# Choosing each expert's first tokens from 512 packed words, a longer lag in a routing pipeline, and a reordered pair of loads, in a two-layer kernel on Trainium2

## What is computed

```python
# block 0
xn = layernorm(x)
s  = two transformer layers (attention, MLP) of xn, per sequence
logits = xn @ router_w.T                      # 64 experts, top 8 of each token
pos = cumsum(onehot, axis=0) - 1              # place of a token in its expert's queue
valid = pos < 64                              # an expert takes its FIRST 64 tokens
g = silu(routed(valid tokens) + shared)
x = x + s * g
# block 1
xn = layernorm(x)
topk_ids = argmax(xn @ gate_w); score = sigmoid(max)   # 32 experts, top 1
order = argsort(topk_ids)                     # tokens sorted by expert
d = grouped_mm(silu(sorted @ wg) * (sorted @ wu), wd)
x = x + linear_attention(xn) * silu(shared(xn) + d[inverse order])
```

## Time and profile before

| | us |
|---|---|
| three runs | 1530.03, 1534.50, 1534.76 (median 1534.5) |
| the profiled execution, its own time | 1530.27 |
| its span, first to last instruction | 1528.4 |
| PE busy | 1209.7 (79%) |
| PE weight loads busy | 912.8 (60%) |
| DVE busy | 1069.0 (70%) |
| ACT busy | 787.0 (51%) |
| POOL busy | 653.9 (43%) |
| mean granted TensorE clock | 0.909 |

### The profile page before, as it was taken

How to read it: one execution, slowest core, us unless ns; L and a number is a source line. 1 busy time by engine, 2 the same in 40 slices (tenths; PEclk the granted TensorE clock), 3 DMA queues, 4 the chain that set the end, 5 groups by cost and what they waited for, 6 DMA issues and landing times. The chain is left out here.

```text
span 1528.4 us, 29193 instructions
## 1 busy us (share of the span) xinstructions
PE 1209.7 (79%) x7783; PEld 912.8 (60%) x7784; DVE 1069.0 (70%) x3641; ACT 787.0 (51%) x2010; POOL 653.9 (43%) x1270
## 2 busy tenths in 40 slices
PE   3999999999600899999999744568888888698883
PEld 2777777778500677777777533346666666355552
DVE  3777777777697677777777367757777777266663
ACT  1666576665300565665665455646666656233331
POOL 3344343443100354554555456714444433155555
PEclk9999999999855999999999855579999999699997
DMA  3432433424100122122122155534444443355552
GB/s 130 143 133 87 143 103 120 139 88 147 40 0 24 42 58 57 39 60 55 39 61 48 18 167 183 164 131 142 144 148 148 154 155 125 99 165 151 161 167 76
DMA packets 159336, 162.58 MB, mean 106 GB/s; under 512 B 21030, under 2 KB 138509, under 8 KB 159296
## 3 DMA queue, kind: packets, MB, share of 16 engines
q1 hardware_dynamic: 144016, 132.98, 27.6%
q0 software_dynamic: 14848, 26.77, 6.3%
q10 hardware_dynamic: 432, 2.38, 0.4%
HBM read 76.33 MB, written 71.04 MB: 96 GB/s over the span
## 5 line engine op out<-in xcount | busy, mean ns | idle before, releaser
L376 ACT ACTIVATE big<-ps,BHS 128x256 f32<-128x256 f32 x256 | 107.0, 470 | 59.6 <-PE ps L253 58.9
L388 ACT ACTIVATE pr<-ps,nmx 128x256 f32<-128x256 f32 x256 | 117.7, 475 | 32.2 <-DVE nmx L435 31.4
L253 PE MATMUL ps<-big,W 128*128 128x256 f32 x512 | 128.3, 395 | 5.7 <-ACT big L381 5.7
L266 PE MATMUL ps<-W,big 128*128 128x128 f32 x1024 | 130.7, 281 | 0.0
L266 PEld LDWEIGHTS ps<-W,big 128*128 128x128 f32 x1024 | 119.4, 192 | 13.8 <-ACT big L376 9.9
L2102 POOL DMA_INDIRECT out<-X,io x96 | 99.8, 1040 | 34.4 <-issue 34.4
L253 PEld LDWEIGHTS ps<-big,W 128*128 128x128 f32 x512 | 94.4, 194 | 26.2 <-ACT big L381 15.6
L435 DVE TENSOR_REDUCE nmx<-ps 128x2 f32<-128x512 f32 x128 | 82.3, 685 | 36.3 <-PE ps L288 36.3
L979 POOL DMA_INDIRECT ffn<-big,si x64 | 93.9, 1467 | 26.6 <-issue 26.6
L1944 PE MATMUL ps<-big,zT 128*128 x192 | 102.7, 617 | 2.4 <-DVE pr L2040 1.0
L2018 ACT ACTIVATE pr<-ps 128x256 f32<-128x256 f32 x96 | 36.8, 383 | 102.9 <-PE ps L1944 101.8
(11 more groups left out here) (244 smaller groups left out, 3370.1 us busy)
## 6 DMA issues: line engine op xcount, KB each, us to landing
srt<-big SPq DMA_DIRECT2D x16, 1584.0 KB, 5.8
X<-srt SPq DMA_DIRECT2D x24, 800.0 KB, 4.7
big<-we SPq DMA_DIRECT2D x16, 768.0 KB, 4.8
rowd<-big SPq DMA_DIRECT2D x32, 272.0 KB, 2.3
big<-x SPq DMA_DIRECT2D x64, 128.0 KB, 2.2
X<-big SPq DMA_DIRECT2D x64, 128.0 KB, 2.1
big<-we SPq DMA_DIRECT2D x16, 384.0 KB, 3.4
X<-srt SPq DMA_DIRECT2D x24, 256.0 KB, 4.8
```

The lines of the kernel that those rows point to most:

```text
L253: last = pe.matmul(pb[2 * g + f // 2][:, f % 2 * S:(f % 2 + 1) * S], W0[:, l, 512 + f * P:512 + (f + 1) * P], zT2[:, g, :], start=True, st ...
L266: last = pe.matmul(pb[4 + g][:, t * C:(t + 1) * C], hT[:, g, f, t * P:(t + 1) * P], W0[:, l, 1024 + f * C:1024 + (f + 1) * C], start=(f == ...
L376: act.activation(hT[:, g, f, :], pb[2 * g + half][:, f % 2 * S:(f % 2 + 1) * S], ACT.Silu, bias=BHS[:, l, f:f + 1], scale=GELU).then_inc(s ...
L388: last = act.activation(pr[:, g, h, t, :], pb[2 * g + h][:, t * S:(t + 1) * S], ACT.Exp, bias=nmx[:, g, h * TPU + t:h * TPU + t + 1], accu ...
```

## The change

Three edits in three stages, and what they need.

1. **Keys to words.** In stage 1 DVE writes only a 0 or 1 in bf16 for each (token, expert), one instruction of 128x256. PE multiplies it (as weights, four of 128x64) by a constant 128x8 matrix `SUM` that packs 16 tokens into one word of 16 bits, and ACT copies 64x32 in place of 128x256. `words` is 64 experts by 512. In `pick` the words that are not 0 get a large number that falls with their index, plus their own value; the 64 first words of each expert are taken (rows of 512), each is split in four parts of 4 bits and the first 64 non-zero parts are taken (rows of 256), each is split in four bits and the first 64 are taken (rows of 256). The 128 partitions and the DMA between halves are gone. `CST` grows by 520 columns, and one small cast makes `SUM`.
2. **Route.** Everything behind the statistics lags one unit more: norm n-2, transposes n-2, logits n-3, ranks n-4, best n-4, score n-4, scaling n-5, save n-3, store n-5; the code after the loop has one more step.
3. **Stage 4.** SP's list issues the row load of j+2 before it waits for `done` of j-2 and issues the tail of j.

```diff
-        early_at, late_at = [HT * P], [0]
+        early_at, late_at = [TOK // 16], [0]
+                dve.tensor_copy(SUM[:, :], CST[:, C_SUM:C_SUM + P // 16])
...
+        new_words = pb[6][0:E0, S:S + 2 * TPU * N_W]          # N_W = P // 16
...
                             pe.wait_ge(s["key"], i + 1)
-                            for t in range(TPU):
-                                last = pe.transpose(pb[6][:, S + t * P:S + (t + 1) * P],
-                                                    kk[:, t, :, :].rearrange("p g e -> p (g e)"), ident)
+                            for g in range(2):
+                                for t in range(TPU):
+                                    last = pe.matmul(new_words[:, (g * TPU + t) * N_W:(g * TPU + t + 1) * N_W],
+                                                     kk[:, g, t, :], SUM[:, :], start=True, stop=True)
...
-                            act.activation(keys[:, bass.ds(S * i, S)], pb[6][:, S:2 * S], ACT.Copy).then_inc(s["keyT"], 1)
+                            act.activation(words.rearrange("e (g w) -> e g w", g=2)[:, :, bass.ds(TPU * N_W * i, TPU * N_W)],
+                                           new_words.rearrange("e (g w) -> e g w", g=2), ACT.Copy).then_inc(s["keyT"], 1)
...
-                            for g, t in units:
-                                last = dve.tensor_scalar(kk[:, t, g, :], rep[:, g, t, :], NEG / 2,
-                                                         CST[:, bass.ds(C_TOKV + TPU * i + HT * g + t, 1)],
-                                                         ALU.is_lt, ALU.mult)
-                            last.then_inc(s["key"], 1)
+                            dve.tensor_scalar(kk[:, :, :, :], rep[:, :, :, :], NEG / 2, None, ALU.is_lt).then_inc(s["key"], 1)
...
-                    largest(lst, keys)
-                    dve.tensor_copy(both[:, 0:CAP], lst[0:E0, :]).then_inc(halves, 1)
-                    dve.drain()
-                    dve.wait_ge(moved, 16)
-                    largest(fin, both[:, :])
+                    def split(bits, above, scale, signed):
+                        dst = work[:, 0:4 * CAP].rearrange("p (w n) -> p w n", n=4)
+                        dve.tensor_copy(li[:, :], lst[:, :])
+                        dve.drain()
+                        for n in range(4):
+                            dve.tensor_scalar(pi[:, :, n], li[:, :], (3 - n) * bits, 2 ** bits - 1,
+                                              ALU.logical_shift_right, ALU.bitwise_and)
...
+                        dve.tensor_scalar(wide[:, :], wi[:, :], above, None, ALU.add)
+                        dve.tensor_copy(part[:, :, :], pi[:, :, :])
+                        dve.drain()
+                        dve.tensor_tensor(dst, wide[:, :].unsqueeze(2).to_broadcast([E0, CAP, 4]),
+                                          CST[0:E0, C_IOTA:C_IOTA + 4].unsqueeze(1).to_broadcast([E0, CAP, 4]), ALU.subtract)
+                        dve.drain()
+                        dve.scalar_tensor_tensor(dst, part[:, :, :], 0.0, dst, ALU.is_gt, ALU.mult)
+                        dve.drain()
+                        if scale > 1:
+                            dve.scalar_tensor_tensor(dst, dst, float(scale), part[:, :, :], ALU.mult, ALU.add)
+                            dve.drain()
+                    dve.scalar_tensor_tensor(work, words, 0.0, CST[0:E0, C_WORD:C_WORD + TOK // 16], ALU.is_gt, ALU.mult)
+                    dve.drain()
+                    dve.scalar_tensor_tensor(work, work, float(2 ** 24), words, ALU.subtract, ALU.add)
+                    dve.drain()
+                    largest(work, -float(2 ** 25))
+                    split(4, 3.0, 16, True)
+                    largest(work[:, 0:4 * CAP], 0.0)
+                    split(1, 4.0, 1, False)
+                    largest(work[:, 0:4 * CAP], 0.0)
...
-                        if started(r, k, 1):
-                            norm(n - 1, (k - 1) % nb)
+                        if started(r, k, 2):
+                            norm(n - 2, (k - 2) % nb)
...
-                        routed = started(r, k, 3) and (not isinstance(r, int) or n - 3 < UNITS)
-                        k3, k4 = (k - 3) % nb, (k - 4) % nb
+                        routed = started(r, k, 4) and (not isinstance(r, int) or n - 4 < UNITS)
+                        k4, k5 = (k - 4) % nb, (k - 5) % nb
                         if routed:
-                            dve.wait_ge(s["logits"], n - 2)
+                            dve.wait_ge(s["logits"], n - 3)
...
                     steps(dve, step)
-                    for k in range(4):
+                    for k in range(5):
                         step(rounds, k, False)
...
-                        if started(r, k, 1):
-                            rows(n - 1, (k - 1) % nb)
                         if started(r, k, 2):
-                            logits(n - 2, (k - 2) % nb)
+                            rows(n - 2, (k - 2) % nb)
                         if started(r, k, 3):
-                            ranks(n - 3, (k - 3) % nb)
+                            logits(n - 3, (k - 3) % nb)
+                        if started(r, k, 4):
+                            ranks(n - 4, (k - 4) % nb)
...
                             j = 2 * q + b
+                            if not last:
+                                sp.wait_ge(s["xTp"], n_t * j + n_t)
+                                load(j + 2, b)
                             if not first:
                                 sp.wait_ge(s["done"], j - 1)
                                 load_tail(j, b)
-                            if not last:
-                                sp.wait_ge(s["xTp"], n_t * j + n_t)
-                                load(j + 2, b)
```

More of the change, by code:

```diff
@@ L61 @@
 C_TILE = 609
-NCST = C_TILE + SORTED_TILES
+C_WORD = C_TILE + SORTED_TILES
+C_SUM = C_WORD + TOK // 16
+NCST = C_SUM + P // 16
 R_KEY, R_X1, R_S1, R_SH, ROWW = C, C + 16, 2 * C + 16, 3 * C + 16, 4 * C + 16
@@ L99, in mixed_layers @@
         big = sb("big", [P, E1 * 768])
-        keys = big[:, 0:HT * P]
+        words = big[0:E0, 0:TOK // 16]
         WE1 = big[:, :].rearrange("p (e f) -> p e f", e=E1)
@@ L834, in pick @@
         def pick():
-            lst = early([P, CAP])
-            both = early([E0, 2 * CAP])
-            fin = early([E0, CAP])
+            lst = early([E0, CAP])
+            work = early([E0, TOK // 16])
+            part = early([E0, CAP, 4])
+            wide = early([E0, CAP])
+            li = early([E0, CAP]).bitcast(I32)
+            wi = early([E0, CAP]).bitcast(I32)
+            pi = early([E0, CAP, 4]).bitcast(I32)
             kf = early([P, E0 // 2])
@@ L850, in _ @@
                     pool.tensor_scalar(W0[:, 1, 1024:1536], W0[:, 1, 1024:1536], 1.0 / GELU, None, ALU.mult)
-                @block.sync
-                def _(sp):
-                    sp.wait_ge(halves, 1)
-                    sp.dma_start(both[:, CAP:2 * CAP], lst[E0:P, :]).then_inc(moved, 16)
-                    sp.wait_ge(moved, 16)
                 @block.tensor
@@ L861, in _ @@
                     for h in range(2):
-                        last = pe.matmul(pb[0][h * CAP:(h + 1) * CAP, 0:E0], fin[:, :], ident[0:E0, 0:E0],
+                        last = pe.matmul(pb[0][h * CAP:(h + 1) * CAP, 0:E0], lst[:, :], ident[0:E0, 0:E0],
                                          start=True, stop=True)
@@ L1249, in _ @@
                     steps(sp, step)
-                    for k in range(2):
-                        save(UNITS - 2 + k, nb - 2 + k)
-                    for k in range(4):
-                        store(rounds - 1, UNITS - 4 + k, nb - 4 + k)
+                    for k in range(3):
+                        save(UNITS - 3 + k, nb - 3 + k)
+                    for k in range(5):
+                        store(rounds - 1, UNITS - 5 + k, nb - 5 + k)
                     for k in range(2):
@@ L1303, in _ @@
                     n = UNITS
-                    norm(n - 1, nb - 1)
-                    for k in range(4):
+                    for k in range(5):
                         if k < 2:
-                            turned(rounds - 1, n - 2 + k, nb - 2 + k)
+                            norm(n - 2 + k, nb - 2 + k)
                         if k < 3:
-                            score(n - 3 + k, nb - 3 + k)
-                        scaled(n - 4 + k, nb - 4 + k)
+                            turned(rounds - 1, n - 3 + k, nb - 3 + k)
+                        if k < 4:
+                            score(n - 4 + k, nb - 4 + k)
+                        scaled(n - 5 + k, nb - 5 + k)
                 @block.vector
@@ L1354, in step @@
                         if routed:
-                            which(k3)
+                            which(k4)
                         dve.drain()
@@ L1367, in step @@
                         if routed:
-                            hot(n - 3, k3)
-                        if started(r, k, 4):
-                            ranked(n - 4, k4)
```

(17 more changed lines are left out.)

56 lines of the change are left out of this document (35 added, 21 removed).

## The result

The changed kernel takes 1470.99 us (median of four runs, 1470.27 to 1472.35), the kernel before 1532.98 beside it: ratio 0.959, 95% interval 0.9574 to 0.9606. It is faster by 4.1%, but it lies 3 us outside the forecast range of 1440 to 1468 and 18 above the forecast of 1453. The profiled execution took 1472.35 us with a span of 1470.5; the one before, 1530.27 and 1528.4. Medians and ratios of this study leave out slow runs, of which there was one, 2074.08 us, of the kernel with DVE's copy first.

What follows compares the result with a forecast made beforehand. Bounds by stage: PE in stage 1, DVE in the pick, a ring in the route, PE's row-load waits in stage 4. 1530.3 - 40.0 + 0.7 - 3 - 12.3 - 24.2 = 1451.5, median put at 1453; range 1440 to 1468.

Steps and rivals of the forecast that it cites:

- allowance of 0.5 for GpSimd's work: Pick: 0.5 us in case GpSimd's preparation of block 1's weights holds DVE up.
- the splits: Pick: small DVE instructions dividing words into parts and bits, 3.55 us for the first and 2.8 for the second.
- Rival 3: Pick and stage 1: strided integer writes and casts dearer, stage 1 at its upper end, +5 and +6.5, 1464; chance 0.07.
- the ring: Route: circular dependency through DVE, POOL, ACT and PE; one passage of 7.2 us paces two steps, three with the lag.
- Rival 1: Route: DVE's two additions block POOL 0.28 us each per unit, step 3.5, gain 1.2, time 1464; chance 0.13.
- a step of 3.8: Route: POOL's step if each DVE addition blocks it for the full 0.43 us, giving 1472.
- 1.5 had been charged: Route: half a step, 1.5 us, for the last step added after the loop.
- 6.6 a chunk: Stage 4: chunk length with loads hidden, down from 7.81 us, giving -24.2 over 20 chunks.
- rival 2: Stage 4: the row load doesn't hide or the tail delays DVE's sum; half the gain left, 1465; chance 0.12.
- the stall: Stage 4: PE's row transpose waits for the row load once a chunk, 1.4 to 1.8 us, 20 times.
- Below, all of the 0.22 goes; above, they cost twice it: Stage 1, PE: packing matmuls replacing two fp32 transposes change an iteration by -0.22 to +0.22 us; -0.1 taken, 16 times.
- 1.4 us from DVE's shorter keys: Stage 1: DVE's 0.74 us becomes 0.3 to 0.43, saving 1.4 of 5.0 us of waits at PE's prob transposes.

Runs made afterwards that it cites:

- kernel with DVE's copy first: Changed kernel, but in stage 4 DVE copies the turned hidden values of tile t-2 ahead of tile t's product: 1459.25 us, 0.9536.
- reordered kernel: Kernel before, lag kept; in the route ACT's copy goes ahead of normalising and PE's logits ahead of the next unit's transposes: 1516.38 us, 0.9908.
- Constant numbers: Changed kernel with constant expert numbers 0 to 7 in stage 4 in place of PE's table load: 1454.04 us in one run, stage 4 185.7.
- early load: Kernel with DVE's copy first, plus PE's table load right behind the gate and up matmul of a chunk's fourth tile: 1453.48 us, 0.9490.
- fillers: Matmuls without a use in PE's three waits ending stage 1; on the changed kernel 8, 3, 3: 1467.17 us; 4, 1, 1: 1464.21 us.

## Why the prediction was wrong

**Pick, right.** 34.6 against 35.8 us, each round as forecast; the allowance of 0.5 for GpSimd's work beside it was not needed, and the splits were a little cheaper. Rival 3 fell for the pick; its other half, stage 1 at the upper end, came and went beyond it.

**Route, right in mechanism, and in size with some luck.** 3.13 us a step for 3.1, -12.4 for -12.3. The reading of the ring was confirmed from the other side, by the reordered kernel. Rival 1 fell: POOL's power instruction has a median of 0.725 us and 0.944 at worst in the new schedule. By the Trainium skill, page "SBUF — State Buffer", section "Who interferes with whom", a step of 3.8 had been worked out; no such step is in the trace, where the longest from step 4 on is 3.6. The end behind the last step grew from 14.05 to 17.8 us, 3.7 where 1.5 had been charged, and the first four steps, 8.6 us in place of 11.6, which were in no term, made up for it: two errors that cancelled.

**Stage 4, the step that failed.** "PE then goes at 1.64 a tile; with the slightly longer first one, 6.6 a chunk". The loads hide as forecast: the row load lands in 3.0 us, the tail in 4.6, and rival 2 fell in its mechanism, though the gain is the half that it named. Two things were wrong in the length of the chunk. First, the step to the chunk's first tile was misread from the trace of before. 6.6 leaves some 0.04 us for it, and the tile that the earlier trace rows show (1496.95 to 1498.59) is of the last chunk, where nothing is late; in the loop the step took 1.73 and 2.03 us by turns, 0.25 above a tile in the mean. Removing the stall alone would have given 6.8 a chunk and about 20 us, so this is 4 of the missing 11.3. Second, that step was taken for a property of the tile. It is a path of its own: DVE's product, its copy, PE's wait, at every second end the branch, the table load of 0.59, the gate and up matmul. It was 0.4 us shorter before only because the stall had given DVE time. With the stall gone, 0.66 us a chunk is exposed: chunk 7.2, and 20 x (7.81 - 7.2) = 12.2, against 12.9 measured. The prediction asked what is late next and looked at POOL, DVE's busy time and DMA, not at the instructions that the page doesn't count as busy. Constant numbers show the whole size, 15.6 us, and the early load gets 14.2 of it back with the numbers kept.

The Trainium skill, page "Runtime: NRT & Kernel Launch", section "Instruction fetch mechanics", gives about 200 ns a register for this instruction, where it loads registers from HBM (the chip's main memory). Here eight registers from a table in SBUF (the on-chip memory) take 0.59 us, 74 ns each, so the figure does not fit this load, and the measured one goes before it; by the page's figure the load would have been 1.6 us, an estimate.

**Stage 1, the second.** "Below, all of the 0.22 goes; above, they cost twice it", with -0.1 an iteration taken, and 1.4 us from DVE's shorter keys. An iteration became 0.19 us longer, near the upper end, 14 x 0.19 = 2.7 us; DVE's key instruction fell from 0.74 us to 0.29, but gave nothing that shows: the wait of the earlier trace rows is gone by its name, and PE's weight loads idle as long at the same line, 5.9 us in place of 5.0 and 1.0, with no wait that the profile names. The second row of that line before, then its row in the changed kernel (us in total, times, longest; both 20 to 380 us):

```profile
PEld ps L297 <- issue: 1.0, 3, 0.4
```

```profile
PEld ps L301 <- issue: 5.9, 16, 0.4
```

The other 3.1 us lie behind the last copy of the words and were in no term: in six of the seven kernels with bf16 words and no fillers the granted clock fell there to 0.50 to 0.53, the 1.2 GHz level, for 5 us or more, and stage 1 lasted 402.0 to 406.3 us, in the seventh it held and it was 399.1; in the kernels with the old transposes it was 397.5 to 398.3. The held clock gives back 2.7 us in the same place with fillers, and where it held by itself 3.0 of the 3.1 are gone, so the clock's part is shown. That the words make the fall dearer is shown by count only: from the last copy to the pick it took 13.4 to 13.6 us at a fallen clock with the old transposes (three kernels) and 15.0 to 16.2 with the bf16 words (six); what in them does it is open (PE's wait there is 1.77 us with them, 1.61 without).

**The range.** Its upper end took in the rivals one at a time. Two terms failed together, by 8.5 and 11.3; either alone would have stayed within it.

## What to carry to other kernels

Where a wait is removed from a steady loop, list what else each engine does between two passages of it, register loads, branches and semaphore waits too, and start every one of them from its own releaser: a stall hides other delays for nothing, and their price appears when it goes. A load of indices to registers belongs where its sequencer waits anyway. Before lengthening a pipeline's lag, look whether an engine's list takes the younger unit ahead of the older one: two swaps took more off the route here than one unit of lag.

## What the runs showed of the hardware

- Eight registers from a table cost PE's sequencer 0.59 us, and cost the kernel up to 15.6 us in 24 chunks although PE was busy in 132.65 of the 140 us from 1300 to 1440.
- Four matmuls of 8 columns (bf16, 64-column weights) took 0.12 us where more of them stood already and 0.41 between a group of 64 and a group of 256 columns in fp32.
- After a PE wait of 1.77 us (1.61 with the old transposes) the granted clock fell from 1.00 to 0.51 in most executions and not in all: in ten of the twelve kernels without fillers, one profile each. In the eight with fillers it held.
- The same program differed by 1.1% between two chips, with late signals of PE on the slower, while the kernel before differed by 0.05% there. A gain of this size wants a second chip before it is believed.
